# Two tiles of the recurrence's keys turned and copied one slice later in the first feed-forward stage

## The chip, the cores and the metric

The kernel runs on 1 core of one Trainium2 chip. The metric is the device time of the program in microseconds (us), the median of three executions. Times inside the program come from the trace of one more, profiled execution; they count from its first instruction.

## What is computed

The input is 8 sequences of 256 rows by 512 columns. Four layers follow, each a mixing part and a feed-forward part, each with a layer norm ahead of it and a gated residual sum behind it. Only two parts matter here. With the gates' tanh left out:

```python
wu, wg, wd = (ternary_quant(w) for w in (W_up, W_gate, W_down))      # first feed-forward part, 512 -> 2048 -> 512
x = x + (silu(norm(x) @ wu.T) * (norm(x) @ wg.T)) @ wd.T

def step(carry, kv_t):                                                # second mixing part, one step of time
    p, q, o = carry
    kt, vt = kv_t
    no = maximum(o, u + kt);  A = exp(o - no);  E = exp(u + kt - no)
    y = (A * p + E * vt) / (A * q + E)
    no2 = maximum(w + o, kt); A2 = exp(w + o - no2); E2 = exp(kt - no2)
    return (A2 * p + E2 * vt, A2 * q + E2, no2), y
x = x + scan(step, keys=norm(x), values=context)
```

The keys of the recurrence are the normed output of the first feed-forward part. The recurrence of a sequence needs that sequence's finished rows and nothing of the other sequences.

## The kernel before

One stage holds both parts and works on the 8 sequences in turn (loop over b). A sequence has two tiles of 128 rows (t_ = 0, 1). The 2048 inner columns are cut into 8 slices of 256 (loop over j). While sequence b goes through the feed-forward part, the recurrence of b-1 begins, that of b-2 is finished, and the result of b-3 is added to the rows.

Five engines run programs of their own, each strictly in the order in which it is written; semaphores join them. The orders are written out by hand, slice by slice.

TensorE does, for each slice j: `up_gate` (L823, 32 matmuls into two banks); the small turns that belong to this slice; from j = 2 on `down(b, j - 2)` (L810, 8 matmuls). After slice 7 come `down(b, 6)` and `down(b, 7)`. A turn is four transposes with the identity. There are three kinds: `y_back` (L833, through bank 1) turns the recurrence's result of b-3 back, tile 0 at j = 0 and tile 1 at j = 2; `keys` (L738) turns the normed rows of b-1, tile 0 at j = 1 and tile 1 at j = 2; `transpose_front` for b+1 (also L738) turns the rows of the next sequence at j = 4 and 6. The last two share bank 0 and wait on `xn_ready` and on `front_bank_free`.

ScalarE does, for each slice: the tanh (L925), the high half of the hidden values (`hid_high`, L928), then what belongs to the slice: `present_exp` at j = 0, `key_copy` (L884, copies a turned key tile out of bank 0) at j = 1 and 2, a sum over a chunk of later weights (`sum_later`, L266), `ffn_high` (L757) at j = 4 and 6, `history_relu` at j = 6.

VectorE does, for each slice: the hidden values (L1060 and L1062, here `hid`), then steps of the norm or the recurrence, then the low half (`hid_low`, L1082), then more steps. At j = 0 it makes the sums of the norm of b-1 (L743, L747) ahead of `hid_low` and applies it (`norm_apply`, L752) behind; at j = 1 there are three products (L983 to L985) and, behind `hid_low`, `add_y` (L1013) for b-3, tile 0; at j = 2 totals (L991, L993) and the sums of the norm of b+1; at j = 3 a reciprocal (L1000), `add_y` for tile 1 and `norm_apply` of b+1; at j = 4 `running_max` (L1022), which waits for both copied key tiles; at j = 5 `differences` (L1033); then scans (L1043, L1052) and the sum into the rows (L1102). The reciprocal square root of each norm (L169, L170) is GpSimd's.

`up_gate(b, j)` waits until `hid` of slice j-2 is done. `y_back` of tile 1 waits until `add_y` of tile 0 has emptied bank 1. For b = 0 there are no keys, for b below 3 no `y_back`, and for b = 7 no norm or turn of a next sequence.

Of the kernel before, what the change touches and what calls it, by code (L numbers as in the profile page):

```python
# [65 lines left out]
def build(nc, t):  # L66
# [3 lines left out]
    with ctx:  # L70
# [45 lines left out]
        def S1(name):  # L116

            k = names.setdefault(name, len(names))
            return sc[:, k:k + 1]
# [4 lines left out]
        def sig(name):  # L124
            if name not in sems:
                sems[name] = sem(name)
            return sems[name]
# [132 lines left out]
        def sum_later(act, n):  # L260

            if n + 1 < len(LATER):
                load_chunk(act, later_no[n + 1], LATER[n + 1][0], LATER[n + 1][1])
            act.wait_ge(*chunk_loaded(later_no[n]))
            buf = staged[later_no[n]][1]
            nc.scalar.activation(buf, buf, LATER[n][2], accum_out=w_sums[:, n:n + 1]).then_inc(sig("stage_free"), 1)  # L266
# [74 lines left out]
        def prep_pe(pe, sub, nm):  # L341
            pe.wait_ge(sig("prep_sums"), PREP_NO[sub])
            nc.tensor.matmul(psum[:, 7, 0:nm], ones[:, :], part[:, SUMS_AT[sub]:SUMS_AT[sub] + nm], start=True, stop=True).then_inc(sig("prep_total"), 1)
# [378 lines left out]
        def front_of_ffn(b):  # L722

            return 8 if b == 0 else 7 + 2 * b

        def front_of_wkv(c):

            return 23 if c == B - 1 else 10 + 2 * c

        def tile_no(f, t_):  # L730

            return f * TT + t_ + 1

        def transpose_front(pe, f, t_):
            pe.wait_ge(sig("xn_ready"), tile_no(f, t_))
            pe.wait_ge(sig("front_bank_free"), tile_no(f, t_))
            for k in range(KD):
                last = nc.tensor.transpose(psum[:, 0, k * P:(k + 1) * P], xn[:, f % 2, t_, k * P:(k + 1) * P], ident[:, :])  # L738
            last.then_inc(sig("xT_ready"), 1)
# [61 lines left out]
        def pe_stage12(pe):  # L801
            def down(b, j):
                for t_ in range(TT):
                    if j == 0:
                        pe.wait_ge(sig("ffn0_added"), b * TT + t_ + 1)
                    if t_ == 0:
                        pe.wait_ge(sig("hid_low_ready"), b * NJ + j + 1)
                    for k in (2 * j, 2 * j + 1):
                        for n, h in enumerate((hTh, hTl)):
                            last = nc.tensor.matmul(psum[:, 6 + t_, :], h[:, k, t_ * P:(t_ + 1) * P], w0_down[:, k, :],  # L810
                                                    start=(k == 0 and n == 0), stop=(k == KE - 1 and n == 1))
                    if j == NJ - 1:
                        last.then_inc(sig("down_ready"), 1)

            def up_gate(b, j):
                pe.wait_ge(sig("hid_ready"), b * NJ + j + 1)
                for side, w in ((0, w0_up), (1, w0_gate)):
                    bank = 2 + 2 * (j % 2) + side
                    for m in (2 * j, 2 * j + 1):
                        out = psum[:, bank, (m % 2) * S:(m % 2 + 1) * S]  # L820
                        for k in range(KD):
                            for n, xt in enumerate((xTh, xTl)):
                                last = nc.tensor.matmul(out, w[:, k, m * P:(m + 1) * P], xt[:, b % 2, k, :],  # L823
                                                        start=(k == 0 and n == 0), stop=(k == KD - 1 and n == 1))
                    last.then_inc(sig("up_gate_ready"), 1)

            def y_back(c, t_):
                if c < 0:
                    return
                pe.wait_ge(sig("wkv_y_ready"), c + 1)  # L830
                pe.wait_ge(sig("wkv_added"), c * TT + t_ + TT)
                for k in range(KD):
                    last = nc.tensor.transpose(psum[:, 1, k * P:(k + 1) * P], wk_y[:, k, t_ * P:(t_ + 1) * P], ident[:, :])  # L833
                last.then_inc(sig("wkv_yT_ready"), 1)

            def keys(c, t_):
                if c >= 0:
                    transpose_front(pe, front_of_wkv(c), t_)

            pe.wait_ge(sig("weights_ready"), 1)  # L840
            for t_ in range(TT):
                transpose_front(pe, front_of_ffn(0), t_)
            for b in range(B):
                f = front_of_ffn(b)
                pe.wait_ge(sig("front_bank_free"), tile_no(f, TT))
                for j in range(NJ):
                    if b == 0 and j < 2:
                        pe.wait_ge(sig("conv_added"), B + 3 + 2 * j)
                    if b == 0 and j == 2:
                        pe.wait_ge(sig("conv_added"), NTILES)  # L850
                    up_gate(b, j)
                    if j == 0:
                        y_back(b - 3, 0)
                    if j == 1:
                        keys(b - 1, 0)
                    if j == 2:
                        y_back(b - 3, 1)
                        keys(b - 1, 1)
                    if j in (4, 6) and b + 1 < B:
                        transpose_front(pe, front_of_ffn(b + 1), j // 2 - 2)  # L860
                    if j >= 2:
                        down(b, j - 2)
                down(b, NJ - 2)
                down(b, NJ - 1)
            y_back(B - 3, 0)
            keys(B - 1, 0)
            y_back(B - 3, 1)
            keys(B - 1, 1)
            for t_ in range(TT):
                y_back(B - 2, t_)  # L870
            prep_pe(pe, 3, 4)
            for t_ in range(TT):
                transpose_front(pe, NEXT, t_)
            for t_ in range(TT):
                y_back(B - 1, t_)

        def act_stage12(act):
            def key_copy(c, t_):
                if c < 0:
                    return  # L880
                act.wait_ge(sig("xT_ready"), tile_no(front_of_wkv(c), t_))
                if c and t_ == 0:
                    act.wait_ge(sig("wkv_eps_ready"), 2 * KD * c)
                nc.scalar.activation(wk_k[:, :, t_ * P:(t_ + 1) * P], psum[:, 0, :].rearrange("p (k n) -> p k n", k=KD),  # L884
                                     ACT.Copy).then_inc(sig("front_bank_free"), 1)
# [25 lines left out]
            def present_exp(c):  # L911
                if c < 0:
                    return
                act.wait_ge(sig("wkv_relu_done"), 4 * (c + 1))
                nc.scalar.activation(wk_d[:, 0:2], wk_d[:, 0:2], ACT.Exp, scale=-1.0).then_inc(sig("wkv_exp_ready"), 1)
# [5 lines left out]
            for b in range(B):  # L921
                for j in range(NJ):
                    n = b * NJ + j
                    act.wait_ge(sig("up_gate_ready"), 2 * n + 1)
                    nc.scalar.activation(th[:, j % 2, :], psum[:, 2 + 2 * (j % 2), :], ACT.Tanh,  # L925
                                         scale=S1("half_up")).then_inc(sig("tanh_ready"), 1)
                    act.wait_ge(sig("hid_ready"), n + 3)
                    nc.scalar.activation(hTh[:, 2 * j:2 * j + 2, :], hid[:, j % 2, :].rearrange("p (m s) -> p m s", m=2),  # L928
                                         ACT.Copy, scale=2.0 ** -26).then_inc(sig("hid_high_ready"), 1)
                    if j == 0:  # L930
                        present_exp(b - 2)
                    if j in (1, 2):
                        key_copy(b - 1, j - 1)
                    if j in (1, 2, 3, 5, 6):
                        sum_later(act, 5 * b + (1, 2, 3, 5, 6).index(j))
                    if j in (4, 6) and b + 1 < B:
                        ffn_high(act, front_of_ffn(b + 1), (b + 1) % 2, j // 2 - 2)
                    if j == 6:
                        history_relu(b - 1)
                    if j == 7:  # L940
                        history_exp(b - 1)
                        present_relu(b - 1)
# [2426 lines left out]
```

## Time and profile before

| | |
|---|---|
| median of 3 executions | 3387.77 us (3387.43 to 3389.38) |
| the profiled execution | 3388.9 us |
| its span, first to last instruction | 3387.1 us |
| TensorE busy | 2922.5 us, 86% |
| VectorE busy | 2494.4 us, 74% |
| ScalarE busy | 1724.4 us, 51% |
| sequence b = 1 in the stage, 401.50 to 447.65 us | 46.15 us |
| b = 2 | 52.48 us |
| b = 3 to 6, each | 53.45 or 53.46 us |
| b = 7 | 50.43 us |

Busy times are sums over stages that have different limits. A sequence is counted here from the first matmul of its `up_gate(b, 0)` to that of the next. In a timeline the duration of a merged row includes the modelled end of its last matmul, which overlaps what follows; the distance between starts tells how long the engine was taken. The bracket at the end of a row is idle time of that engine before it, and what ended it.

### The profile page before, as it was taken

The numbers are of one execution on the slowest core, as the hardware profiler recorded it, in microseconds if no ns is written. First come the engines' busy times: TensorE is split into PE (matmuls) and PEld (weight loads), VectorE is DVE, ScalarE is ACT, GpSimd is POOL, SyncE is SP. The second block draws the span as 40 slices with busy tenths as digits, with TensorE's granted clock in tenths as the row PEclk, the third lists the DMA queues.
The fourth block names the chain that finished last, engine by engine and source line by source line (L and its number), as shares of the span: only waits on it lengthen the run. The fifth ranks groups of instructions, "written<-read, shape, count | busy, mean of one in ns | idle before, by whom it ended". The sixth has DMA issues, their size and how long they took to land.

```text
span 3387.1 us, 49017 instructions
## 1 busy us (share of the span) xinstructions
PE 2922.5 (86%) x18354; PEld 1703.4 (50%) x18354; DVE 2494.4 (74%) x4562; ACT 1724.4 (51%) x2661; POOL 921.8 (27%) x1361
## 2 busy tenths in 40 slices
PE   7899998892788888768888667999999999988998
PEld 3344666661444444456666433545555455544665
DVE  6787589988766667688888768777777777766333
ACT  3222344444355555179998864444445444454443
POOL 4554000001300000046776774222222222211000
PEclk9999999995999999889999878999999999999999
DMA  6422212121110102100000021000000000021000
GB/s 235 139 91 84 59 55 64 55 63 70 41 32 23 26 17 72 43 31 1 1 1 1 28 92 39 7 1 7 1 7 7 1 7 7 1 72 32 13 19 19
DMA packets 52651, 132.62 MB, mean 39 GB/s; under 512 B 6416, under 2 KB 19536, under 8 KB 51152
## 3 DMA queue, kind: packets, MB, share of 16 engines
q1 hardware_dynamic: 43216, 96.11, 9.0%
q10 hardware_dynamic: 9216, 33.56, 3.3%
q8 instruction: 141, 2.31, 0.3%
q14 instruction: 78, 0.64, 0.1%
HBM read 119.03 MB, written 4.19 MB: 36 GB/s over the span
## 4 chain that ended last, share of the span: by engine, by line
PE 49%; DVE 24%; issue 12%; ACT 9%; POOL 4%; DMA 1%; SPq 0%; DVEq 0%; ACTq 0%; POOLq 0%
PE psum L1263 10%; PE psum L652 6%; PE psum L2231 5%; PE psum L2761 3%; PE psum L2720 3%; ACT area_g L2306 3%; PE psum L823 3%; PE psum L2112 2%; PE psum L2745 2%; PE psum L2730 2%; PE psum L2252 2%; DVE area_a L1870 2%; PE psum L1518 2%; PE psum L1499 2%; DVE xn L3018 1%
## 5 line engine op out<-in xcount | busy, mean ns | idle before, releaser
L2306 ACT ACTIVATE area_g<-area_a 128x2048 bf16<-128x2048 f32 x168 | 334.8, 1997 | 31.4 <-POOL area_a L2175 22.2
L2231 PE MATMUL psum<-area_c,ident_bf 128*128 128x128 bf16 x3328 | 234.2, 236 | 94.1 <-DVE area_c L2340 94.1
L652 PE MATMUL psum<-area_b,area_g 128*128 128x512 f32 x640 | 284.8, 600 | 6.4 <-DVE x_stream L547 3.6
L169 POOL TENSOR_TENSOR rstd<-mean_var,eps_col 128x2 f32<-128x2 f32 x57 | 19.2, 336 | 980.7 <-DVE mean_var L747 497.1
L2231 PEld LDWEIGHTS psum<-area_c,ident_bf 128*128 128x128 bf16 x3328 | 219.1, 107 | 119.9 <-DVE area_c L2340 112.7
L2720 PE MATMUL psum<-area_b,stage 128*128 128x512 f32 (+1 forms) x512 | 237.9, 547 | 0.0
L823 PE MATMUL psum<-xT_high,area_a 128*128 128x256 f16 x1024 | 234.7, 278 | 1.4 <-DVE xT_low L762 1.4
L823 PE MATMUL psum<-xT_low,area_a 128*128 128x256 f16 x1024 | 234.3, 278 | 0.0
L2872 ACT ACTIVATE xn<-psum,small 128x384 f32<-128x384 f32 (+1 forms) x256 | 163.5, 639 | 96.0 <-DVE small L3011 95.8
L3011 DVE TENSOR_REDUCE small<-psum 128x1 f32<-128x384 f32 (+1 forms) x256 | 158.0, 617 | 72.2 <-PE psum L2721 70.4
L2637 POOL TENSOR_TENSOR small<-small,half_pow 128x4 f32<-128x4 f32 x96 | 131.7, 1372 | 273.8 <-DVE small L2958 273.8
L652 PEld LDWEIGHTS psum<-area_b,area_g 128*128 128x128 f32 x640 | 121.0, 192 | 156.0 <-issue 143.8
L2745 PE MATMUL psum<-area_g,area_a 128*128 128x512 f16 x672 | 166.2, 381 | 29.4 <-DVE area_g L3024 24.3
L2881 ACT ACTIVATE area_g<-psum 128x384 f16<-128x384 f32 (+1 forms) x256 | 139.2, 544 | 93.1 <-PE psum L2730 91.4
L2171 POOL TENSOR_SCALAR area_a<-area_a 128x1 f32<-128x1 f32 x224 | 129.1, 576 | 184.5 <-ACT area_g L2306 175.9
L2629 POOL TENSOR_TENSOR stage<-area_g 128x256 f32<-128x256 f32 x79 | 58.6, 742 | 441.1 <-ACT area_g L2854 311.7
L1263 PE MATMUL psum<-area_c,xT_high 128*128 128x512 f16 x512 | 178.6, 390 | 0.0
L1870 DVE TENSOR_REDUCE area_a<-psum 128x2 bf16<-128x512 f32 x256 | 163.3, 681 | 15.8 <-PE psum L1477 15.4
L470 POOL TENSOR_TENSOR area_b<-area_b,area_c 128x512 f32<-128x512 f32 x128 | 137.8, 1107 | 117.5 <-PE psum L652 109.8
L3017 DVE RECIPROCAL small<-small 128x1 f32<-128x1 f32 x256 | 41.6, 163 | 167.9 <-ACT xn L2872 165.0
L2730 PE MATMUL psum<-ident,xn 128*128 128x128 f32 x896 | 145.5, 279 | 19.8 <-DVE xn L3018 19.0
L3024 DVE SCALAR_TENSOR_TENSOR area_g<-psum,area_g 128x384 f16<-128x384 f32 (+1 forms) x256 | 157.8, 616 | 0.8 <-ACT area_g L2881 0.8
(423 smaller groups left out, 7493.3 us busy)
## 6 DMA issues: line engine op xcount, KB each, us to landing
stage<-in_w ACTq DMA_DIRECT2D x24, 512.0 KB, 4.3
stage<-in_w SPq DMA_DIRECT2D x24, 512.0 KB, 3.7
area_g<-in_toeplitz SPq DMA_DIRECT2D x32, 256.0 KB, 2.6
area_b<-in_ctxT SPq DMA_DIRECT2D x15, 512.0 KB, 3.9
area_b<-area_b SPq DMA_DIRECT2D x24, 256.0 KB, 3.7
stage<-in_ctxT SPq DMA_DIRECT2D x9, 512.0 KB, 3.9
x_stream<-in_x SPq DMA_DIRECT2D x4, 1024.0 KB, 12.2
area_c<-in_ctxT SPq DMA_DIRECT2D x4, 1024.0 KB, 11.2
```

Source lines behind the costliest of these rows:

```text
L652: last = nc.tensor.matmul(psum[:, bank + m, :], toep[:, h % 2, (m - k) * P:(m - k + 1) * P], kv[:, h % 2, k, :], start=(k == 0), stop=(k = ...
L823: last = nc.tensor.matmul(out, w[:, k, m * P:(m + 1) * P], xt[:, b % 2, k, :], start=(k == 0 and n == 0), stop=(k == KD - 1 and n == 1))
L1263: r = nc.tensor.matmul(out, u, v, start=(first and n == 0), stop=(last_ and n == 2))
L1870: nc.vector.tensor_reduce(max4[:, st % 2, 4 * u + 2 * n:4 * u + 2 * n + 2], src, AX.X, ALU.max, negate=True).then_inc(sig("max4_ready"), 1)
L2231: last = nc.tensor.matmul(psum[:, 1, t_ * P:(t_ + 1) * P], identb[:, :], above5[:, t_, c * P:(c + 1) * P], start=(c == 0), stop=(c == KE - 1))
L2306: nc.scalar.activation(junk5[t_], z5[b % 3][:, t_, :], ACT.Sign, bias=fine5[:, par, t_:t_ + 1], scale=-1.0, accum_out=signs5[:, t_:t_ + 1] ...
L2720: nc.tensor.matmul(psum[:, 2 + n % 2, 0:nk], qT6[:, u % 2, h, :], kT6[:, b % 2, 0:nk // P, g, :], start=True, stop=False)
L2730: last = nc.tensor.transpose(psum[:, 4 + n % 2, k * P:(k + 1) * P], p6[:, n % 2, k * P:(k + 1) * P], ident[:, :])
L2745: last = nc.tensor.matmul(psum[:, 6, :], v6[:, b % 2, k, vp, g * P:(g + 1) * P], pT6[:, pp, k, :], start=(vp + pp + k == 0), stop=(pp == 1 ...
L2872: nc.scalar.activation(p6[:, n % 2, 0:nk], psum[:, 2 + n % 2, 0:nk], ACT.Exp, bias=nmax6[:, n % 2:n % 2 + 1], scale=-1.0, accum_out=sum6[: ...
L3011: nc.vector.tensor_reduce(nmax6[:, n % 2:n % 2 + 1], psum[:, 2 + n % 2, 0:nk], AX.X, ALU.min).then_inc(sig("nmax6_ready"), 1)
L3024: nc.vector.scalar_tensor_tensor(out=pT6[:, 1, 0:nb, h * P:(h + 1) * P], in0=psum[:, 4 + n % 2, 0:nb * P].rearrange("p (n q) -> p n q", q= ...
```

## The change

On TensorE the turn of key tile 0 moves from slice 1 to slice 2, behind `y_back` of tile 1, and that of tile 1 from slice 2 to slice 3, behind `up_gate(b, 3)` and ahead of `down(b, 1)`. On ScalarE the copies move from slices 1 and 2 to slices 2 and 3. Nothing is added or taken away.

```diff
@@ pe_stage12 @@
                     up_gate(b, j)
                     if j == 0:
                         y_back(b - 3, 0)
-                    if j == 1:
-                        keys(b - 1, 0)
                     if j == 2:
                         y_back(b - 3, 1)
-                        keys(b - 1, 1)
+                    if j in (2, 3):
+                        keys(b - 1, j - 2)
                     if j in (4, 6) and b + 1 < B:
                         transpose_front(pe, front_of_ffn(b + 1), j // 2 - 2)
@@ act_stage12 @@
                     if j == 0:
                         present_exp(b - 2)
-                    if j in (1, 2):
-                        key_copy(b - 1, j - 1)
+                    if j in (2, 3):
+                        key_copy(b - 1, j - 2)
                     if j in (1, 2, 3, 5, 6):
                         sum_later(act, 5 * b + (1, 2, 3, 5, 6).index(j))
```

## Rows read from the trace of the kernel before

**Rows 1.** What TensorE waited for, 350 to 800 us: total, times, longest.

```profile
PE psum L738 <- DVE xn L752: 36.3, 13, 9.1
PE psum L833 <- DVE x_stream L1013: 9.1, 6, 3.5
```

**Rows 2.** Timeline of TensorE in b = 5: start, duration, line, [idle before].

```profile
614.36 0.27 PE L823 MATMUL psum<-xT_low,area_a 128*128 128x256 f16 x1
617.70 0.66 PE L738 MATMUL psum<-ident,xn 128*128 128x128 f32 x4 [3.07 <-DVE xn L752]
...
621.58 0.27 PE L823 MATMUL psum<-xT_low,area_a 128*128 128x256 f16 x1
624.24 0.63 PE L833 MATMUL psum<-ident,area_g 128*128 128x128 f32 x4 [2.38 <-DVE x_stream L1013]
624.70 0.60 PE L738 MATMUL psum<-ident,xn 128*128 128x128 f32 x4
625.14 1.89 PE L810 MATMUL psum<-area_a,area_b 128*128 128x512 f16 x8
...
637.01 0.66 PE L738 MATMUL psum<-ident,xn 128*128 128x128 f32 x4 [1.27 <-DVE xn L752]
```

**Rows 3.** Timeline of VectorE in b = 5.

```profile
617.10 1.00 DVE L752 TENSOR_SCALAR xn<-x_stream,mean_var,rstd 128x512 f32<-128x512 f32 x2 [0.87 <-POOL rstd L170]
...
623.35 0.74 DVE L1013 SCALAR_TENSOR_TENSOR x_stream<-psum,gates,x_stream 128x512 f32<-128x512 f32 x1
...
630.63 0.69 DVE L1060 SCALAR_TENSOR_TENSOR area_b<-area_b,psum 128x512 f32<-128x512 f32 x1 [0.76 <-PE psum L823]
...
636.42 0.99 DVE L752 TENSOR_SCALAR xn<-x_stream,mean_var,rstd 128x512 f32<-128x512 f32 x2
...
642.99 0.69 DVE L1060 SCALAR_TENSOR_TENSOR area_b<-area_b,psum 128x512 f32<-128x512 f32 x1 [1.34 <-PE psum L823]
```

**Rows 4.** Timelines of TensorE and VectorE in b = 1.

```profile
408.38 0.27 PE L823 MATMUL psum<-xT_low,area_a 128*128 128x256 f16 x1
410.31 0.66 PE L738 MATMUL psum<-ident,xn 128*128 128x128 f32 x4 [1.66 <-DVE xn L752]
...
431.10 0.69 DVE L1060 SCALAR_TENSOR_TENSOR area_b<-area_b,psum 128x512 f32<-128x512 f32 x1 [1.32 <-PE psum L823]
```

**Rows 5.** Timelines of TensorE, VectorE and ScalarE in b = 2.

```profile
454.53 0.27 PE L823 MATMUL psum<-xT_low,area_a 128*128 128x256 f16 x1
...
454.94 0.69 DVE L1062 TENSOR_TENSOR area_b<-area_b,psum 128x512 f32<-128x512 f32 x1
...
459.26 1.11 PE L738 MATMUL psum<-ident,xn 128*128 128x128 f32 x4 [4.45 <-DVE xn L752]
...
465.17 0.69 DVE L1060 SCALAR_TENSOR_TENSOR area_b<-area_b,psum 128x512 f32<-128x512 f32 x1 [0.19 <-PE psum L823]
...
467.15 0.58 ACT L884 ACTIVATE area_b<-psum 128x512 f32<-128x512 f32 x1
```

**Rows 6.** Timeline of VectorE in b = 7.

```profile
743.32 0.67 DVE L1060 SCALAR_TENSOR_TENSOR area_b<-area_b,psum 128x512 f32<-128x512 f32 x1
...
747.97 0.69 DVE L1060 SCALAR_TENSOR_TENSOR area_b<-area_b,psum 128x512 f32<-128x512 f32 x1 [0.32 <-PE psum L823]
```

**Rows 7.** Timeline of ScalarE in b = 5.

```profile
625.97 0.58 ACT L884 ACTIVATE area_b<-psum 128x512 f32<-128x512 f32 x1
...
634.03 0.69 ACT L925 ACTIVATE area_b<-psum,scalars 128x512 f32<-128x512 f32 x1 [0.29 <-PE psum L823]
```

**Rows 8.** Stretches of b = 6: busy us of each engine, PEclk the granted clock.

```profile
669.00:671.00 2.00, 0.00 (x0) 0.00 (x0) 1.14 (x4) 1.56 (x2) 1.24 (x2) 0.98 0.00 0
671.00:673.00 2.00, 1.85 (x9) 1.54 (x10) 1.97 (x5) 0.10 (x1) 0.00 (x0) 0.50 0.04 8
```

**Rows 9.** Timeline of TensorE in b = 4, and behind b = 7.

```profile
565.25 0.42 PE L823 MATMUL psum<-xT_high,area_a 128*128 128x256 f16 x1
...
568.45 0.31 PE L823 MATMUL psum<-xT_low,area_a 128*128 128x256 f16 x1
...
808.22 1.09 PE L833 MATMUL psum<-ident,area_g 128*128 128x128 f32 x4 [9.46 <-DVE x_stream L1013]
```

## The prediction

> **What bounds the kernel now.** The change touches one stage, so I read the waits of TensorE over the stage first [rows 1], then the timelines of the engines for each sequence. The waits show what the change aims at: TensorE idled 36.3 us for normed rows (13 times) and 9.1 us for `add_y`. A wait is worth its length only if the engine that ended it isn't the one that ends the next wait too, so the timelines decide.
>
> In b = 5 TensorE is through with `up_gate(b, 1)` at 614.6 and stands until 617.70, when VectorE has applied the norm; it does the key turn and `up_gate(b, 2)`, is done at 621.85, and stands again until `add_y` ends, 624.24 [rows 2]. VectorE waits 0.87 us for GpSimd, starts `norm_apply` at 617.10 and then has no idle time until 630.63, where it waits 0.76 us for `up_gate(b, 3)` [rows 3]. `add_y`, which frees `y_back`, lies in the middle of this unbroken run. So the path goes: VectorE from 617.10 to 624.1, TensorE from 624.24 (`y_back`, key turn, `down(b, 0)`, `up_gate(b, 3)`) to 630.36, VectorE from 630.63 to the normed rows of b+1 at 636.9, TensorE from 637.01 on, VectorE again at 642.99 after a wait of 1.34 us [rows 2, 3]. The first key turn lies beside VectorE's run and is not on this path. The start of `y_back` repeats in b = 3 to 7 with steps of 53.45 or 53.46 us, so all five run in this way.
>
> **Removing the wait at slice 1, b = 3 to 7.** The turn goes, and TensorE can begin `up_gate(b, 2)` at 614.5, since `hid` of slice 0 is done at 614.0. It ends at about 618.1 (3.5 us, 32 matmuls at 0.109 us from start to start). Then it stands for `add_y`, whose time VectorE sets: 624.24 as before. Two stalls of 3.07 and 2.38 us have become one of 6.1 us; gain 0. Behind it the other key turn stands in the same place, so `up_gate(b, 3)` starts as before: 0.
>
> **The turn added at slice 3.** It takes 0.44 us (624.70 to 625.14 [rows 2]) and delays `down(b, 1)` and `up_gate(b, 4)`. In b = 3 to 6 the wait of 1.27 us for the normed rows of b+1 follows [rows 2] and takes it in. In b = 1 the turn only changes its place inside a TensorE-bound run. In b = 7 there is no such wait: `hid` of slice 4 begins at 743.32 without idle time, 0.6 us behind the end of `up_gate`, which hides the turn, but slice 5 waits for TensorE by 0.32 us, and everything behind follows it [rows 6]. That is +0.44 us, once. If the cover in b = 3 to 6 were gone, it would be 4 x 0.44 = 1.8 us more.
>
> **b = 1.** There is no `y_back` here, and VectorE idles for TensorE at slices 3, 4 and 5, as at 431.10 [rows 4]. The last matmul before the stall starts at 408.38 and the turn at 410.31, where 0.11 would do: 1.83 us lost [rows 4]. After the change the rows (ready at 410.2) are there when the turn is reached at 412.0. TensorE keeps this lead to slice 5, from which the rest of the sequence hangs. -1.83 us.
>
> **b = 2.** The stall is the largest, 4.45 us [rows 5], but little of it comes back. `up_gate(b, 2)` waits for `hid` of slice 0, whose second half begins at 454.94 and ends at 455.6 [rows 5], so it starts at 455.7 instead of 460.2. VectorE runs without idle time from `norm_apply` on to slice 2, where it waits 0.19 us for TensorE [rows 5]; that is the gain. From there to the normed rows of b+1 it has no idle time at all. Here the second key turn meets a new wait: it needs bank 0, which `key_copy` empties behind `hid_high` of slice 2, at about 467.4 (the copy that stands there today starts at 467.15 and takes 0.48 to its successor [rows 5]; 0.19 us earlier than that), while TensorE is through with `up_gate(b, 3)` at 464.9. TensorE stands 2.5 us, then needs 5.7 us to the end of `up_gate(b, 4)`, 473.1, still ahead of the normed rows at 476.6. Price 0 as long as that lead of 3.5 us lasts. b = 2: -0.19 us.
>
> **ScalarE.** Each copy takes 0.48 to 0.58 us. The copy of tile 0 now follows `hid_high` of slice 2, at 625.97, just where the copy of tile 1 stood there [rows 7], and its tile is turned by 625.14. The copy of tile 1 falls at 632.6 to 633.1, ahead of `running_max` at 638.64, and pushes the tanh of slice 4 from 634.03 [rows 7] to about 634.5, against 637.33 for the `hid` that needs it. Price 0; without that cover 0.5 us for each of seven sequences, 3.4 us. No DMA's order changes, and the loads issued behind the copies feed sums that nobody waits for in this stage.
>
> **TensorE's clock.** The one 6.1 us stall is not the same as the two that it replaces. In b = 6 the granted clock falls to 0.50, the lower level of 1.2 GHz, as work resumes after a stall of 3.07 us, [rows 8] and is back by 674.3. In b = 4 it falls 4.0 us after TensorE stopped at 561.2 and stays low from 565.25 to 568.45 [rows 9]. In b = 2, 3, 4, 6 and 7 such a stretch of 3.0 to 3.4 us follows the stall; in b = 5 there is none. Today it hits `up_gate(b, 2)`, which takes up to 1.7 us longer and ends before `add_y` even so (570.06 against 570.78 in b = 4): it costs nothing. After the change the work behind the stall is `y_back`, key turn, `down(b, 0)` and `up_gate(b, 3)`, 6.12 us that lie wholly on the path (624.24 to 630.36). Each microsecond at the lower level there costs half a microsecond. The trace has no 6.1 us stall in the loop. Lower bound 0, if the fall came and went inside the stall; with the times of b = 4 (low from 4.0 to 7.3 us after the stop) 1.2 us would be left, cost 0.6. All of a stretch costs 3.3 / 2 = 1.7; one and a third would cost 2.2. Behind a stall of 9.46 us the four transposes start low and take 1.09 us against 0.63 [rows 9, 2], so I take it that the clock is always low at the return, and the middle of 0.6 and 1.7, rounded: 1.2 us for each of five, 6.0 us (0 to 11).
>
> The Trainium skill, page "TensorE: Matmul & The Clock Gate", section "HAM oscillation — how this bites in real kernels", says that a loop which waits too long in each turn starts cold every time and pays half of the throttled time. By that rule all five restarts pay in full, the fourth rival below; the trace agrees on the half (matmuls 0.213 against 0.109 us apart) but not on every time, since b = 5 kept its clock.
>
> **The sum.** -1.83 - 0.19 + 0.44 + 6.0 = +4.4 us. On the profiled execution, 3388.9 us (its span of 3387.1 and 1.8 around it), that gives 3393.3. The median of the runs is 1.1 us lower, 3387.77, and gives 3392.2 us. A change can be told from none from about 0.2%, 6.8 us, on.
>
> **The rivals.**
>
> 1. The forecast: VectorE's run keeps `y_back` where it is, and the clock takes more than b = 1 gives. 3392.2 us; with 0.6 to 1.7 us for each restart, 3389 to 3395. Chance 0.62.
>
> 2. The clock costs nothing on the path: the low stretch passes inside the stall, as the clock also held in b = 5. Then -1.6 us, 3386.2. Against it: of the six stalls of 3 us or more in the loop five ended low or fell within 1.0 us of the return. Chance 0.14.
>
> 3. The stalls at slice 1 are worth their length: 1.83 + 4.6 + 5 x 3.1 = 21.9 us, 3365.9. For it speaks only the sum of waits [rows 1]. Against it: VectorE would have to reach `add_y` earlier, and it waits for nothing of TensorE's between 617.10 and 630.63 [rows 3]. Chance 0.05.
>
> 4. The other side: each of the five restarts pays a whole low stretch or more, 1.7 to 2.2 us, 8.5 to 11 us, less 1.6: +6.9 to +9.4, 3394.7 to 3397.2 us. It decides from 1.7 us a restart. For it: the fall in b = 6 came exactly at the return, and the clock is granted by what the engine did before, which is now 6.1 us of nothing. Against it: a stretch that began 4.0 us after the stop, as in b = 4, is in part spent. Chance 0.14.
>
> 5. ScalarE's copy in slice 3 lands on the path and adds up to 3.4 us to the forecast: 3395.6. Against it the 2.8 us between the new tanh and its user. Chance 0.05.
>
> **How the numbers follow.** The time is that of case 1. The range of 8 in 10 leaves out rival 3 and the outer tails: from just under rival 2 (3385.8) to the top of rival 4 (3397.2), rounded. Faster by over 0.2% is rival 3 and a little of an unseen gain: 0.07. Slower by over 0.2% (above 3394.5) is rival 4, part of rival 5 and the edge of case 1: 0.21. Within it 0.72. Case 1's own range is 3389 to 3395.
>
> **What would show it.** In the profile after: in b = 3 to 7 no idle time before `up_gate(b, 2)` and one stall of about 6.1 us before `y_back` at slice 2, ended by `add_y` (L1013); the granted clock low just behind it; the distance between sequences 53.46 us plus 0.6 to 1.7; a length of 44.3 us for b = 1; a new wait of some 2.5 us for `key_copy` in b = 2; the waits for normed rows of b+1 down from 1.27 to about 0.8. The prediction is wrong if `y_back` at slice 2 moves earlier against VectorE's `norm_apply`, if the clock stays high, or if VectorE shows a new wait for ScalarE at slice 4.

## The result: 0.29% slower

| | before | changed |
|---|---|---|
| median of 9 executions each | 3387.91 us (3386.98 to 3392.43) | 3397.32 us (3396.83 to 3399.52) |
| ratio, 95% interval | | 1.0029 (1.0019 to 1.0039) |
| span of the profiled execution | 3387.1 us | 3395.1 us |
| b = 1 to 7 in the stage | 362.89 us | 371.84 us |

The kernel is 9.4 us slower. The forecast was +4.4 us (3392.2), with a range up to 3397.2; the measured time is just above the range. The median is also above the 0.2% line, though the lower end of the interval, 0.19%, reaches just below that line.

The waits of TensorE over the stage (350 to 810 us of the changed kernel, columns as in [rows 1]) show that the change did what it aims at, and where the wait went. Lines behind the edit have moved up by one: L1012 is `add_y`, L883 `key_copy`.

```profile
PE psum L833 <- DVE x_stream L1012: 34.1, 6, 6.1
...
PE psum L738 <- DVE xn L752: 13.7, 6, 9.1
PE psum L738 <- ACT area_b L883: 2.5, 1, 2.5
```

The wait for normed rows fell by 22.6 us, that for `add_y` rose by 25.0. The new wait for `key_copy` (the line with L883) came once, in b = 2, and was 2.5 us.

The timelines of TensorE and VectorE in b = 5 of the changed kernel, beside [rows 2, 3]:

```profile
627.64 1.09 PE L833 MATMUL psum<-ident,area_g 128*128 128x128 f32 x4 [6.12 <-DVE x_stream L1012]
628.51 1.06 PE L738 MATMUL psum<-ident,xn 128*128 128x128 f32 x4
629.37 2.63 PE L810 MATMUL psum<-area_a,area_b 128*128 128x512 f16 x8
...
635.33 0.60 PE L738 MATMUL psum<-ident,xn 128*128 128x128 f32 x4
```
```profile
620.50 1.00 DVE L752 TENSOR_SCALAR xn<-x_stream,mean_var,rstd 128x512 f32<-128x512 f32 x2 [0.86 <-POOL rstd L170]
...
626.75 0.74 DVE L1012 SCALAR_TENSOR_TENSOR x_stream<-psum,gates,x_stream 128x512 f32<-128x512 f32 x1
...
635.60 0.69 DVE L1059 SCALAR_TENSOR_TENSOR area_b<-area_b,psum 128x512 f32<-128x512 f32 x1 [2.33 <-PE psum L823]
```

Three distances are to be read here. From `norm_apply` to `add_y` VectorE takes 6.25 us, as before (617.10 to 623.35), so taking the first wait away moved nothing on VectorE. The two stalls have become one of 6.12 us. And from the start of `y_back` to that of the next turn (the end of `up_gate(b, 3)`) TensorE takes 7.69 us where it took 6.12; VectorE's wait at slice 3 goes from 0.76 to 2.33 us by the same 1.57.

The granted clock of the changed kernel in the same place (columns as in [rows 8], the granted clock is the last column but two):

```profile
621.00:623.00 2.00, 0.52 (x5) 0.21 (x3) 1.97 (x5) 0.14 (x1) 0.00 (x0) 1.00 0.00 0
623.00:625.00 2.00, 0.00 (x0) 0.00 (x0) 2.00 (x2) 2.00 (x4) 0.00 (x0) 0.76 0.53 117
625.00:627.00 2.00, 0.00 (x0) 0.00 (x0) 2.00 (x4) 0.10 (x1) 0.00 (x0) 0.50 0.37 150
627.00:629.00 2.00, 1.36 (x7) 1.39 (x8) 1.97 (x4) 0.16 (x1) 0.00 (x0) 0.50 0.64 182
629.00:631.00 2.00, 2.00 (x8) 0.94 (x7) 2.00 (x3) 1.86 (x3) 0.00 (x0) 0.54 0.47 117
631.00:633.00 2.00, 2.00 (x16) 1.42 (x15) 1.88 (x4) 0.24 (x2) 0.00 (x0) 1.00 0.65 225
```

The clock falls inside the stall, at about 624, and stays at the lower level of 1.2 GHz until about 630.9. That is 6.8 us, twice the stretches of 3.4 us in the kernel before, and 3.2 us of it lie behind the return.

The same for all five sequences, each from the start of `y_back` to the end of `up_gate(b, 3)`, in b = 3 to 7:

```profile
515.98:524.87 8.89, 8.89 (x49) 6.16 (x50) 5.45 (x9) 2.95 (x5) 0.89 (x2) 0.68 0.39 119
572.21:580.30 8.09, 8.09 (x48) 5.89 (x49) 5.45 (x9) 2.95 (x5) 0.89 (x2) 0.75 0.45 131
627.64:635.33 7.69, 7.69 (x49) 5.81 (x49) 5.45 (x9) 2.95 (x5) 0.89 (x2) 0.79 0.45 135
682.67:690.15 7.48, 7.48 (x48) 5.75 (x49) 5.45 (x9) 2.95 (x5) 0.89 (x2) 0.81 0.47 139
737.49:746.56 9.07, 9.07 (x49) 6.25 (x50) 4.01 (x5) 2.95 (x5) 0.00 (x0) 0.67 0.38 117
```

At full clock this work takes 6.12 us. The share of the clock that is missing, times the length (0.32 of 8.89 us, and so on), is 2.8, 2.0, 1.6, 1.4 and 3.0 us, and that is what each row is longer than 6.12, to 0.1 us.

The stage by sequences, from the changed kernel's trace (busy us of TensorE, its weight loads, VectorE, ScalarE and GpSimd, then the granted clock):

```profile
402.29:446.57 44.28, 43.67 (x337) 32.98 (x336) 29.07 (x53) 21.52 (x34) 2.14 (x4) 1.00 0.20 60
446.57:498.78 52.21, 46.07 (x337) 33.12 (x336) 48.28 (x71) 25.45 (x38) 2.13 (x4) 0.97 0.21 61
498.78:555.01 56.23, 47.74 (x346) 35.10 (x345) 48.77 (x72) 24.84 (x37) 2.14 (x4) 0.94 0.18 57
555.01:610.44 55.43, 46.94 (x345) 34.83 (x344) 48.76 (x72) 24.83 (x37) 2.14 (x4) 0.94 0.20 58
610.44:665.48 55.04, 46.54 (x346) 34.73 (x345) 48.78 (x72) 24.84 (x37) 2.14 (x4) 0.94 0.19 58
665.48:720.30 54.82, 46.33 (x346) 34.71 (x345) 48.77 (x72) 24.83 (x37) 2.14 (x4) 0.94 0.20 59
720.30:774.13 53.83, 46.82 (x338) 34.39 (x337) 44.62 (x63) 23.26 (x35) 1.24 (x2) 0.94 0.16 49
```

b = 1 and 2 got shorter by 1.87 and 0.27 us, b = 3 to 7 longer by 2.77, 1.98, 1.58, 1.36 and 3.40 us. Together that is +8.95 us.

### The profile page after: what moved, and what is told of

It is laid out like the page before. It is cut to its first block, busy times and chain, and to the rows that moved or that the text cites. A ratio compares the mean times of both kernels' runs of the same rounds, so it can differ in the third digit from the quotient of the medians.

```text
span 3395.1 us, 49017 instructions
## 1 busy us (share of the span) xinstructions
PE 2925.3 (86%) x18354; PEld 1705.0 (50%) x18354; DVE 2495.1 (73%) x4562; ACT 1724.9 (51%) x2661; POOL 922.0 (27%) x1361
## 4 chain that ended last, share of the span: by engine, by line
PE 49%; DVE 24%; issue 12%; ACT 9%; POOL 4%; DMA 1%; SPq 0%; DVEq 0%; ACTq 0%; POOLq 0%
PE psum L1262 10%; PE psum L652 6%; PE psum L2230 5%; PE psum L2760 3%; PE psum L2719 3%; ACT area_g L2305 3%; PE psum L823 3%; PE psum L2111 2%; PE psum L2744 2%; PE psum L2729 2%; PE psum L2251 2%; DVE area_a L1869 2%; PE psum L1517 2%; PE psum L1498 2%; PE psum L810 1%
## 5 line engine op out<-in xcount | busy, mean ns | idle before, releaser
L2305 ACT ACTIVATE area_g<-area_a 128x2048 bf16<-128x2048 f32 x168 | 334.7, 1996 | 31.8 <-POOL area_a L2174 22.6
```

The source lines that it names most:

```text
L2305: nc.scalar.activation(junk5[t_], z5[b % 3][:, t_, :], ACT.Sign, bias=fine5[:, par, t_:t_ + 1], scale=-1.0, accum_out=signs5[:, t_:t_ + 1] ...
```

## The experiments

The whole times alone can't tell most of these kernels apart. What lies outside b = 1 to 7, which no kernel here changes, took between 3018 and 3028 us in the profiled executions, and the executions of one kernel spread over 3 to 17 us. That scatter goes with the granted clock: over 106 executions of the kernel before, the middle time is 3381.6 us where the mean clock of the span was 0.953 and 3391.2 us where it was 0.949. So each kernel is read first by the length of its sequences in the trace, which is that of one execution, then by its time. "Changed" and "before" in a name tell from which of the two kernels it was made; all others were made from the changed one. The sequences are counted as before, b = 7 to the next turn of `y_back`. Each ratio is to executions of the kernel before taken with that kernel, whose median lay between 3387.2 and 3389.4 us. All in us:

| kernel | b=1 | 2 | 3 | 4 | 5 | 6 | 7 | sum | median | ratio to before |
|---|---|---|---|---|---|---|---|---|---|---|
| before | 46.15 | 52.48 | 53.46 | 53.45 | 53.46 | 53.46 | 50.43 | 362.89 | | |
| changed | 44.28 | 52.21 | 56.23 | 55.43 | 55.04 | 54.82 | 53.83 | 371.84 | 3397.32 | 1.0029 (1.0019 to 1.0039) |
| full filler | 44.28 | 52.21 | 53.44 | 53.45 | 53.46 | 53.46 | 50.89 | 361.19 | 3383.56 | 0.9991 (0.9982 to 1.0000) |
| half filler | 44.28 | 52.23 | 56.36 | 55.14 | 55.14 | 54.99 | 52.23 | 370.37 | 3397.64 | 1.0027 (1.0017 to 1.0036) |
| first three | 44.28 | 53.89 | 53.44 | 53.45 | 53.46 | 53.45 | 50.44 | 362.41 | 3386.63 | 0.9995 (0.9986 to 1.0004) |
| last five | 46.16 | 53.26 | 55.51 | 55.06 | 54.85 | 56.41 | 52.95 | 374.20 | 3396.99 | 1.0029 (1.0018 to 1.0041) |
| tile 1 alone | 46.16 | 52.49 | 53.02 | 53.02 | 53.01 | 53.02 | 50.85 | 361.57 | 3387.55 | 1.0002 (0.9993 to 1.0011) |
| before, one filler | 46.16 | 52.51 | 55.14 | 53.46 | 55.15 | 55.15 | 51.93 | 369.50 | 3390.58 | 1.0003 (0.9994 to 1.0012) |
| before, two fillers | 46.16 | 53.29 | 53.46 | 53.45 | 53.45 | 53.46 | 50.44 | 363.71 | 3382.92 | 0.9987 (0.9977 to 0.9998) |
| changed, all filled | 44.27 | 52.21 | 53.44 | 53.45 | 53.45 | 53.45 | 50.89 | 361.16 | 3389.27 | 1.0007 (0.9998 to 1.0015) |
| down first | 44.28 | 53.88 | 53.94 | 52.61 | 52.96 | 52.73 | 48.72 | 359.12 | 3384.28 | 0.9983 (0.9974 to 0.9992) |
| arranged | 44.28 | 53.89 | 54.28 | 54.28 | 53.38 | 52.59 | 48.72 | 361.42 | 3386.65 | 0.9993 (0.9984 to 1.0002) |
| down first, filled | 44.27 | 53.89 | 54.26 | 54.25 | 54.25 | 52.57 | 48.72 | 362.21 | 3388.36 | 1.0000 (0.9992 to 1.0009) |
| the same, slice 4 too | 44.28 | 52.21 | 52.57 | 52.58 | 52.56 | 52.58 | 48.72 | 355.50 | 3383.67 | 0.9993 (0.9984 to 1.0001) |

### Full filler: work in the stall

```diff
+            def fill(b, n):
+                for _ in range(n):
+                    nc.tensor.matmul(psum[:, 0, 0:S], w0_up[:, 0, 0:P], xTh[:, b % 2, 0, :], start=True, stop=True)
...
                     if j == 2:
+                        if b >= 3:
+                            fill(b, 46)
                         y_back(b - 3, 1)
```

> The changed kernel with 46 matmuls more, of 256 columns each, between up_gate of slice 2 and y_back of tile 1 in b = 3 to 7. They go into bank 0, which is free there, and nothing reads them. At 0.109 us each they fill 5.0 of the 6.1 us for which TensorE stands. Theory (the clock): with work in the stall the granted clock stays at 1.00 behind it, y_back to the end of up_gate(b, 3) takes 6.1 us again instead of 7.5 to 9.1, VectorE's wait at slice 3 goes from 2.3 us in b = 5 back to 0.76, and the 10.7 us that the five sequences lost come back: 3386.7 us. Rival (the moved turns and copies): the loss comes from what now stands in slice 3 and on ScalarE; the filler changes nothing of that and the time stays at 3397 us, or rises.

TensorE and VectorE in b = 5 (here L1018 is `add_y`, L1065 the first half of `hid`), and two of the sequences:

```profile
615.67 5.19 PE L838 MATMUL psum<-xT_high,area_a 128*128 128x256 f16 x46
621.95 0.63 PE L833 MATMUL psum<-ident,area_g 128*128 128x128 f32 x4 [1.09 <-DVE x_stream L1018]
...
628.34 0.69 DVE L1065 SCALAR_TENSOR_TENSOR area_b<-area_b,psum 128x512 f32<-128x512 f32 x1 [0.76 <-PE psum L823]
```
```profile
604.75:658.21 53.46, 49.99 (x391) 38.24 (x390) 48.77 (x72) 24.72 (x37) 2.14 (x4) 1.00 0.19 60
...
711.67:762.56 50.89, 48.89 (x383) 37.46 (x382) 44.62 (x63) 23.15 (x35) 1.25 (x2) 1.00 0.18 52
```

With 46 matmuls of dead work in the stall the clock stays at 1.00, the wait of VectorE is 0.76 us to the hundredth, and b = 3 to 6 are as long as before the change. b = 7 keeps +0.46 us, the turn in slice 3. So the fall of the clock accounts for 10.65 us of the stage (371.84 - 361.19), and the rest is -1.87 - 0.27 + 0.46. In this run the moved turns and copies stand where they stand in the changed kernel and cost 0.46 us in all, so they are not the cause of the loss. The median, 3383.56 us, is 3.1 below what was expected, which is within the scatter.

### Half filler

```diff
-                            fill(b, 46)
+                            fill(b, 23)
```

> As the first kernel with a filler, with 23 matmuls, 2.5 us, instead of 46; TensorE then stands 3.6 us ahead of y_back. Theory (the clock): the clock falls in some of the five sequences and not in others, as it did behind the stalls of 3.07 us, so the time lies between the full filler's 3386.7 and the changed kernel's 3397.3 us, about 3391 us. Rival (moved turns and copies): 3397 us.

A miss in size: 370.37 us, nearly the changed kernel. TensorE still stood 3.60 us in each of the five, and the clock fell each time, in b = 4 and 5 only after the return (0.8 and 0.3 us). The low stretch was 6.8 us in b = 3 and 3.4 us in the others, but next to all of a 3.4 us stretch now lay behind the return. The five cost 9.2 us against 10.65 for the 6.1 us stall: a stall shorter by two fifths was cheaper by only a seventh.

### First three and last five sequences

```diff
-                    if j in (2, 3):
-                        keys(b - 1, j - 2)
+                    if b < 3 and j in (2, 3) or not b < 3 and j in (1, 2):
+                        keys(b - 1, j - 2 if b < 3 else j - 1)
```

The copies on ScalarE follow the same condition; the other kernel has `b >= 3` in its place.

> The new order for b below 3 alone, the old one for b = 3 to 7. Theory (the clock): only b = 1 and 2 gain, 1.9 and 0.3 us as the trace of the changed kernel shows them; there are no 6.1 us stalls: 3385.8 us. Rival (moved turns and copies cost in every sequence): two sevenths of the 9.4 us, 3390.5 us.

> The new order for b = 3 to 7 alone, the old one for b below 3. Theory (the clock): the loss is all here, 10.7 us and 0.4 us for the turn in b = 7, without the gain of b = 1 and 2: 3399 us, and more or less by 2 us as the low stretches fall otherwise. Rival (moved turns and copies cost in every sequence): five sevenths of 9.4 us, 3394.6 us.

The loss of the changed kernel goes with b = 3 to 7: +10.5 us there with the last five moved (their sum is 274.78 against 264.26, the turn in b = 7 included), 0.0 with the first three. (With the last five moved, b = 2 is 0.8 us longer too, in its old order: the low stretch at its 4.45 us stall was 6.8 us there and 3.4 in the kernel before.) With the first three moved, b = 1 gives its 1.87 us. b = 2 does not do what was expected: 53.89 us, 1.68 more than in the changed kernel with the same order. This time the clock did not fall behind the new wait for `key_copy` (2.47 us). So TensorE came earlier to slice 4, stood 2.93 us there ahead of the next turn, and the clock was low behind that stall:

```profile
476.00 1.06 PE L738 MATMUL psum<-ident,xn 128*128 128x128 f32 x4 [2.93 <-DVE xn L752]
```

In the changed kernel the clock fell behind the wait for `key_copy`, in time that b = 2 has to spare: the low stretch shortened the stall at slice 4 to 1.24 us and cost nothing else.

### Tile 1 alone

```diff
-                    if j in (2, 3):
-                        keys(b - 1, j - 2)
+                    if j in (1, 3):
+                        keys(b - 1, j // 2)
```

> Tile 0 of the keys stays in slice 1; tile 1 alone moves, from slice 2 to slice 3, on both engines. Theory (the clock): the stalls stay two (3.1 us and 0.7 to 2.4 us), so a fall of the clock still lies in up_gate(b, 2), which ends ahead of add_y. Behind y_back there is one turn less, 0.44 us, on the path in b = 3 to 6; in b = 7 it comes back in slice 3. 3387.9 - 1.8 = 3386.1 us. Rival (the turn and the copy in slice 3 cost): this kernel has both of them and shows most of the 9.4 us, 3394 us or more.

Half of the change, with the turn and the copy of slice 3 that the rival blames. b = 3 to 6 are 0.44 us shorter each, the one turn that no longer stands behind `y_back`. b = 7 is 0.42 longer, where 0 was expected, and the trace shows why: the low stretch at the first stall was 6.8 us there (722.7 to 729.5), `up_gate(b, 2)` ended late, and `y_back` began at 730.34 without a wait, 6.95 us behind the key turn instead of 6.53. So the cover over a fall in `up_gate(b, 2)` holds for a stretch of 3.4 us and not quite for one of 6.8. The whole time can't tell 1.3 us.

### The kernel before with fillers

```diff
                     if j == 1:
+                        if b >= 3:
+                            fill(b, 20)
                         keys(b - 1, 0)
```

> Null control: the kernel before, with 20 matmuls of 256 columns (2.2 us) in the 3.1 us stall ahead of the key turn of tile 0 in b = 3 to 7. Theory (the clock only counts on the path): the clock no longer falls in up_gate(b, 2), but that ended ahead of add_y anyway: no change, 3387.9 us within 1.5 us. Rival (a low clock costs wherever it falls, half of its length): four stretches of some 3.2 us come back, 6.5 us, 3381.5 us.

This was meant as a null control and was none: the stage took 369.50 us, +6.6. The filler kept the clock up in `up_gate(b, 2)`, and it fell one stall later, behind the 2.38 us wait for `add_y`, in four of the five:

```profile
517.38 1.03 PE L833 MATMUL psum<-ident,area_g 128*128 128x128 f32 x4 [2.38 <-DVE x_stream L1019]
518.20 1.06 PE L738 MATMUL psum<-ident,xn 128*128 128x128 f32 x4
519.06 2.79 PE L810 MATMUL psum<-area_a,area_b 128*128 128x512 f16 x8
```

In the kernel before, a low `up_gate(b, 2)` had shortened that second stall to 0.7 to 0.9 us. The fall behind the first stall, which cost nothing, had kept the second stall from costing. To make sure, both stalls were filled (the second through bank 6):

```diff
+                    if b >= 3 and j in (1, 2):
+                        fill(b, 20, 0 if j == 1 else 6)
                     if j == 1:
                         keys(b - 1, 0)
```

> The kernel before with 20 matmuls of 256 columns (2.2 us) in each of its two stalls in b = 3 to 7: ahead of the key turn in slice 1 (bank 0) and behind up_gate of slice 2 (bank 6, free until down). It settles why a filler in the first stall alone made the stage 6.6 us longer (369.5 against 362.9 us for b = 1 to 7). Theory (a fall on the path): that filler only moved the falls of the clock from up_gate(b, 2), which has room, to the work behind the 2.38 us stall, which has none; with both stalls filled the clock never falls, each sequence is 53.45 us again and b = 1 to 7 take 362.9 us. Rival (the filler itself costs, by its issue or by the delay of the key turn): b = 1 to 7 take 369 us or more.

b = 3 to 6 took 53.45 or 53.46 us each and b = 7 50.44 us, as before. The filler costs nothing of its own; the place of the fall decides. (b = 2, which has no filler here, was 0.8 us longer behind its own low stretch, hence 363.71.)

### The changed kernel, all filled

```diff
+                    if b >= 3 and j == 2:
+                        fill(b, 46)
+                    if b == 2 and j == 3:
+                        fill(b, 20, 1)
```

> The changed kernel with the full filler in b = 3 to 7 and 20 matmuls (2.2 us, bank 1) in the new 2.5 us wait for key_copy in b = 2. Theory: no fall of the clock from b = 1 to 7; b = 1 to 7 take 361.2 us, as with the full filler alone (there b = 2 took 52.21 us without it; where the fall of the clock comes later in b = 2 it took 53.89). Rival (a moved turn or copy costs): above 363 us.

361.16 us: the clock stays at 1.00 from b = 1 to 7, and the order of the change is worth 1.7 us. Yet the median of this kernel was 1.3 us above that of before and its profiled span 3388.1 us, with 3027 us outside these sequences. The kernel with the full filler has the same stage to 0.03 us and came out at 0.9991 against 1.0007 here. So ratios of whole times differ by 0.16% where the stage is the same.

### Orders that use the stall

First, real work in it:

```diff
-                    if j == 2:
-                        y_back(b - 3, 1)
                     if j in (2, 3):
                         keys(b - 1, j - 2)
+                    if j == 2:
+                        down(b, 0)
+                        y_back(b - 3, 1)
...
-                    if j >= 2:
+                    if j >= 3:
                         down(b, j - 2)
```

> The changed kernel, and in slice 2 the key turn of tile 0 and down(b, 0) stand ahead of y_back of tile 1 instead of behind it. Theory (the clock on the path): 2.2 us of work move into the stall, which shrinks from 6.1 to 3.9 us, and only y_back and up_gate(b, 3), 3.9 us, follow it. VectorE is ready for slice 3 at 5.6 us behind the start of y_back, so up to 1.7 us of a low clock are covered, and the 0.76 us wait of before can go too: between 3380 us (no fall on the path) and 3386 us (half of the falls cost 1 us). Rival (moved turns and copies): the turn and the copy in slice 3 are unchanged; at most 5 x 0.44 us come back, 3395 us.

359.12 us, 12.7 below the changed kernel and 3.8 below before; the ratio is 0.9983 (0.9974 to 0.9992), and this is the only order without dead work whose interval lies below 1. That the program as a whole is 0.17% faster is not shown by it: the kernel before with two fillers, whose stage is 0.8 us longer, came out at 0.9987. The clock still fell at the stall of 3.95 us in four of the five sequences, but `y_back` and `up_gate(b, 3)` now have time to spare: b = 4 to 6 are at most 0.4 us above the 52.57 us that the last kernel below takes without a fall. In b = 3, where the low stretch was 6.8 us, it was 1.4 us.

> The new order for b below 3; in b = 3 to 7 tile 0 of the keys in slice 1, tile 1 in slice 3, and down(b, 0) ahead of y_back of tile 1. Theory: b = 1 and 2 give 2.1 us; in b = 3 to 7 the stalls stay two, a fall of the clock lies in up_gate(b, 2) and down(b, 0), and up_gate(b, 3) ends before VectorE is ready for slice 3, so its wait of 0.76 us goes (2.35 us in b = 7, of which some 1.2): 3387.9 - 2.1 - 4 x 0.76 - 1.2 = 3381.6 us. Rival (turn and copy in slice 3 cost): 3390 us or more.

This keeps tile 0 in slice 1 for b = 3 to 7, has tile 1 in slice 3 and the same early `down(b, 0)`. 361.42 us where 6.3 less than before, 356.6, were expected: b = 3 and 4 took 54.28. Then the fillers were added to the kernel with `down` first (30 matmuls ahead of the key turn in b = 3 to 7, 20 in b = 2):

> Turn and down(b, 0) ahead of y_back, and in front of them 30 matmuls as filler (3.3 of the 3.95 us stall), with the filler of b = 2 as well. Theory: the clock never falls, VectorE's wait at slice 3 is gone in each of b = 3 to 7: 44.3 + 52.2 + 4 x 52.7 + 48.7 = 356.0 us for b = 1 to 7, against 362.9 before, 359.1 without the fillers and 371.8 in the changed kernel. The whole: some 7 us below before, 3381 us. Rival (the wait of VectorE at slice 3 has another cause, such as the tanh): 359 us.

A miss again, 362.21 us, and both had the same main reason. In b = 2, 3 and 4 of the one and b = 2 to 5 of the other the clock falls at slice 4, where TensorE, now earlier, stands longer for the normed rows of b+1, ahead of `down(b, 2)` and `up_gate(b, 5)`, which have nothing to spare. (In the arranged kernel it still fell at the first stall in b = 5 and 6, for 6.8 us in b = 5, which cost 0.8 us there.) The kernel with fillers, b = 3:

```profile
529.74 0.44 PE L738 MATMUL psum<-ident,xn 128*128 128x128 f32 x2 [2.12 <-DVE xn L752]
...
530.26 3.54 PE L810 MATMUL psum<-area_a,area_b 128*128 128x512 f16 x8
```
```profile
529.00:531.00 2.00, 1.26 (x6) 0.79 (x7) 1.97 (x5) 0.00 (x0) 0.00 (x0) 0.79 0.00 0
531.00:533.00 2.00, 2.00 (x6) 0.76 (x5) 2.00 (x4) 1.11 (x2) 0.00 (x0) 0.50 0.00 0
```

So that stall got a filler too, once bank 0 is free:

```diff
+                    if j == 4 and 2 <= b < B - 1:
+                        pe.wait_ge(sig("front_bank_free"), tile_no(front_of_ffn(b + 1), 0))
+                        fill(b, 14)
                     if j in (4, 6) and b + 1 < B:
                         transpose_front(pe, front_of_ffn(b + 1), j // 2 - 2)
```

> As the kernel with turn and down(b, 0) ahead of y_back and the fillers there and in b = 2, and with 14 matmuls (1.5 us) more in the stall at slice 4, ahead of the turn of the next sequence's rows, in b = 2 to 6. It settles why that kernel's sequences took 53.9 and 54.25 us where 52.2 and 52.6 were expected. Theory: the clock fell behind the stalls of 2.9 us (b = 2) and 2.1 us (b = 3, 4, 5) at slice 4, and down(b, 2) and up_gate(b, 5), which lie on the path, paid 1.7 us each time. With work in the stall no fall is left: 44.3 + 52.2 + 4 x 52.6 + 48.7 = 355.6 us for b = 1 to 7, the whole some 7 us below before. Rival (the earlier down or the filler costs in another way, such as by delaying hid of slice 5): 54.2 us a sequence stay, 362 us.

355.50 us against 355.6 expected; each of b = 3 to 6 takes 52.56 to 52.58 us. The clock is at 1.00 throughout. The stage is 7.4 us shorter than before and 16.3 shorter than in the changed kernel. It is also 5.7 us shorter than in the changed kernel with all filled, which is what the turn and `down(b, 0)` ahead of `y_back` are worth. The median, 3383.67 us, is 3.6 below that of before on the same chip, with an interval (0.9984 to 1.0001) that just holds 1. By its stage it is the shortest of all; by whole times that gain is not shown.

## Why the prediction was wrong

**What bounds the stage** was right. In b = 3 to 7 VectorE sets `add_y`, from `norm_apply` on to 6.25 us later, and the removed wait came back behind `up_gate(b, 2)` as 6.1 us in one piece, as was worked out. The wait for the normed rows of b+1 is 0.83 us in b = 5, where 0.8 was forecast.

**b = 1, b = 2 and the turn in b = 7**: -1.83, -0.19 and +0.44 forecast, -1.87, -0.27 and +0.46 measured (b = 7 from the filled kernel). The new wait for `key_copy` in b = 2 was forecast at 2.5 us and was 2.46. **ScalarE** cost nothing: with the clock held up, the stage is as long as these three terms make it.

**TensorE's clock** is the step that failed, in size: the term of 6.0 us measured 10.6. The prediction said "the middle of 0.6 and 1.7, rounded: 1.2 us for each of five, 6.0 us (0 to 11)". The five cost 2.77, 1.98, 1.58, 1.36 and 2.94 us (3.40 less the turn), together 10.63 us, and 10.65 by the kernel with the full filler: 4.6 more than the 6.0, the whole difference between +4.4 and what came, but for the 0.4 us by which whole and stage differ. The mechanism was right, all five restarts came back low, and the upper bound of 11 us held it. What was wrong is that a low stretch was taken to be as long as those of the kernel before, about 3.3 us, so that a long stall would use up a good part of it. In all five the clock was low for 6.8 us. The stall did use up a part, 0.8 to 4.0 us, but 2.8 to 6.0 us were left behind the return. The old stretches came to an end while TensorE was at work in all but their first 0.3 us; here the stall went on into the low stretch, and the stretch went on with it. (That the one is the reason of the other fits every trace here, as the last section shows, but is my reading; no run was made to vary it alone.) That a low stretch is "in part spent" by the stall was the argument against rival 4, which had a chance of 0.14. It was true, and worth too little: rival 4 (3394.7 to 3397.2 us, 8.5 to 11 us for the five) is what happened in the stage, and three of five restarts cost more than 1.7 us.

That a page of the Trainium skill, "TensorE: Matmul & The Clock Gate" in "HAM oscillation — how this bites in real kernels", lets each turn of a waiting loop start cold and pay half of the throttled time was weighed against b = 5 of the kernel before, which had kept its clock. In the changed kernel the trace agrees with the rule five times out of five: 1.57 us lost in b = 5 for 3.2 us at the lower clock behind the return. It does not in every loop: in b = 7 of the kernel with `down` first the clock stayed at 1.00 behind a stall of 3.95 us.

**The sum with the sizes measured**: -1.87 - 0.27 + 0.46 + 10.63 = +8.95, which is 371.84 - 362.89 us in the stage. The median rose by 9.4; the span rose by 8.0, since other parts of the program vary by some microseconds. (Rival 3 counted the stall of b = 2 as 4.6 us, which [rows 5] have as 4.45; nothing hangs on it.)

What the prediction didn't see at all is that the kernel before was sheltered by its first stall. A fall in `up_gate(b, 2)` cost nothing and at the same time shortened the second stall; take the first stall away, as the control with one filler did without moving a turn, and the fall moves onto the path.

## What to carry to other kernels

Where TensorE waits for another engine in each turn of a loop, two stalls with covered work between them can be better than one of the same total, because the clock falls behind a stall and the work behind the last one pays. The cover must be long enough: here a low stretch of 3.4 us was hidden and one of 6.8 us cost 0.4 to 0.8 us. Before a wait is taken away, look for the engine that ends the next one, and ask what stands behind it without room. If a stall can't be avoided, move work that is ready from behind the wait to ahead of it, and check the next stall too: the earlier TensorE arrives there, the longer it stands.

## What the runs showed of the hardware

The clock fell behind shorter stalls than the kernel before suggests. Behind 2.38 us it fell in four of five sequences of the control with one filler; behind 2.12 us in three of four of the kernel with `down` first and fillers (slice 4 of b = 3, 4 and 5, not 6). And it can hold behind a longer one: with `down` first, TensorE stood 3.95 us in b = 7 and the clock stayed at 1.00, where it had fallen in b = 3 to 6. So with the same stall in the same loop it fell in one sequence and not in the next. With no more than 1.7 us of idle time at a stretch (2.9 us once, in b = 2 of the changed kernel with all filled) it stayed at 1.00 in every sequence.

The price of a return isn't fixed either. Ten stalls of 6.1 us are on record, five in the changed kernel and five in the one with the last five moved. The trace's record of the clock gives, in us:

| | b=3 | 4 | 5 | 6 | 7 |
|---|---|---|---|---|---|
| changed: fall, after TensorE stopped | 4.9 | 3.3 | 2.5 | 2.1 | 5.3 |
| low behind the return | 5.7 | 4.0 | 3.2 | 2.8 | 6.0 |
| sequence longer by | 2.77 | 1.98 | 1.58 | 1.36 | 2.94 |
| last five: fall, after TensorE stopped | 3.5 | 2.6 | 2.1 | 5.3 | 3.5 |
| low behind the return | 4.2 | 3.3 | 2.8 | 6.0 | 4.2 |
| sequence longer by | 2.05 | 1.61 | 1.39 | 2.95 | 2.06 |

(b = 7 without the turn, 0.46 us.) The low stretch was 6.8 us in all ten. So the price is half of what is left of it at the return, and the later the clock falls in the stall, the dearer it is. Why it falls at 2.1 us once and at 5.3 another time was not tried.

The length of a low stretch went with where it began. In b = 1 to 7 of all fourteen kernels in the table it lasted 6.8 us where the clock fell 0.8 us or more ahead of the return, whatever the stall (3.07 us in the arranged kernel, 3.60 with half filler), and 3.4 us where it fell less than 0.7 us ahead of the return, at it or behind it. At 0.7 us there is one of each.
